# A decoder layer's long convolution: taps loaded once for two units, part of its products in three reduced-precision parts, and GpSimd's sum one unit later

## The reference

```python
x = x + attention(layernorm(x), qkv_w, qkv_b, out_w, out_b, sinks)
q_ = layernorm(x).reshape(B, T, 512) seen as (batch, 32 heads, 8, 512); k_ = v_ = ctx likewise
kv = einsum('bhil,bhjl->bijhl', k_, v_)
y = irfft(rfft(kv, 1024) * rfft(ssm_kernel, 1024))[..., :512]     # causal convolution along l
out = einsum('bijhl,bhil->bjhl', y + kv * D[head], q_)
x = x + out
x = x + (layernorm(x) @ sum_r factors[r]) / sqrt(8) + bias
```

## Time and profile before

| | us |
|---|---|
| median of 3 runs (1989.84 to 1991.06) | 1990.8 |
| time of the profiled execution | 1991.15 |
| its span in the trace | 1989.3 |
| PE busy in the span | 1945.1 |
| DVE busy | 1549.4 |
| ACT busy | 932.2 |
| POOL busy | 826.0 |

### The profile page before, as it was taken

One profiled execution on the slowest core, in us unless ns is written; L12 is line 12 of the kernel. 1 busy time (PEld: TensorE's weight loads), 2 busy tenths in 40 slices (PEclk: granted clock), 3 DMA queues, 4 the chain that ended last, 5 costly groups with the idle time before them and its releaser, 6 DMA issues.

```text
span 1989.3 us, 44846 instructions
## 1 busy us (share of the span) xinstructions
PE 1945.1 (98%) x15500; PEld 1601.7 (81%) x15500; DVE 1549.4 (78%) x4948; ACT 932.2 (47%) x3481; POOL 826.0 (42%) x947
## 2 busy tenths in 40 slices
PE   6899999999999999999999999999999999999899
PEld 6688888888888888888888888888887777777687
DVE  5777777777777777777777777777777899999887
ACT  4554555555555555555555555555544222222333
POOL 3444434333333333333333333333332666666554
PEclk9999999999999999999999999999999999999999
DMA  6146211111112122121111111111104533333343
GB/s 213 46 118 142 72 54 55 65 54 55 55 54 75 44 97 76 55 89 62 54 55 54 54 54 55 54 65 54 54 33 167 183 103 93 93 93 93 106 142 121
DMA packets 71538, 162.20 MB, mean 82 GB/s; under 512 B 6656, under 2 KB 15232, under 8 KB 71184
## 3 DMA queue, kind: packets, MB, share of 16 engines
q1 hardware_dynamic: 62720, 142.48, 21.4%
q0 software_dynamic: 3840, 8.39, 2.3%
q10 hardware_dynamic: 4752, 8.46, 1.1%
HBM read 108.96 MB, written 50.41 MB: 80 GB/s over the span
## 4 chain that ended last, share of the span: by engine, by line
PE 91%; DVE 3%; issue 2%; ACT 2%; POOL 1%; DMA 0%; DVEq 0%; SPq 0%; ACTq 0%; POOLq 0%
PE banks L534 22%; PE banks L596 18%; PE banks L1180 16%; PE banks L573 9%; PE banks L549 9%; PE banks L559 6%; PE banks L1408 5%; PE banks L527 4%; ACT pr L673 1%; PE banks L484 1%; PE banks L1398 1%; PE banks L473 1%; PE banks L1392 1%; DVE pr L891 1%; DVE m L867 0%
## 5 line engine op out<-in xcount | busy, mean ns | idle before, releaser
L673 ACT ACTIVATE pr<-pr,mx 128x128 f32<-128x128 f32 x1024 | 399.0, 391 | 353.1 <-DVE mx L891 353.0
L752 POOL TENSOR_TENSOR m<-m,rope_sb 128x512 f32<-128x512 f32 x160 | 206.3, 1289 | 513.9 <-ACT m L660 513.9
L534 PE MATMUL banks<-xTh,wh 128*128 128x256 f32 x1280 | 376.4, 294 | 2.3 <-DVE xTl L851 1.4
L534 PE MATMUL banks<-xTl,wh 128*128 128x256 f32 x1280 | 363.0, 284 | 0.0
L534 PE MATMUL banks<-xTh,wl 128*128 128x256 f32 x1280 | 362.6, 283 | 0.0
L1180 PE MATMUL banks<-kv,tap 128*128 128x288 f32 x1280 | 318.4, 408 | 4.3 <-issue 1.5
L1180 PEld LDWEIGHTS banks<-kv,tap 128*128 128x128 f32 x1280 | 238.1, 190 | 83.9 <-issue 23.3
L534 PEld LDWEIGHTS banks<-xTh,wh 128*128 128x128 f32 x1280 | 246.2, 192 | 4.0 <-DVE xTl L851 1.8
L900 DVE TENSOR_TENSOR den<-ac,es 128x4 f32<-128x4 f32 x256 | 51.7, 202 | 253.9 <-ACT es L676 253.7
L534 PEld LDWEIGHTS banks<-xTl,wh 128*128 128x128 f32 x1280 | 246.5, 193 | 0.0
L534 PEld LDWEIGHTS banks<-xTh,wl 128*128 128x128 f32 x1280 | 246.1, 192 | 0.0
(11 more groups left out here) (110 smaller groups left out, 3825.6 us busy)
## 6 DMA issues: line engine op xcount, KB each, us to landing
tap<-padded_taps SPq DMA_DIRECT2D x64, 256.0 KB, 3.3
kk<-in_ctxt SPq DMA_DIRECT2D x64, 192.0 KB, 3.4
x_in<-in_x SPq DMA_DIRECT2D x16, 512.0 KB, 3.8
xt_split<-xTh SPq DMA_DIRECT2D x16, 512.0 KB, 2.6
xt_split<-xTl SPq DMA_DIRECT2D x16, 512.0 KB, 3.6
xb<-in_x SPq DMA_DIRECT2D x16, 512.0 KB, 4.6
factors<-in_factors POOLq DMA_DIRECT2D x8, 1024.0 KB, 8.6
x_part_rows<-x SPq DMA_DIRECT2D x16, 512.0 KB, 3.0
```

The lines of the kernel that those rows point to most:

```text
L534: last = pe.matmul(bank[:, h * T:(h + 1) * T], w[:, n, c, h * P:(h + 1) * P], a[:, s, c, :], start=(c == 0 and i == 0), stop=(c == KD - 1 ...
L673: act.activation(pr[:, s, a, cols], pr[:, s, a, cols], ACT.Exp, bias=mx[:, s, i:i + 1], scale=-1.0, accum_out=ac[:, s, i:i + 1])
L752: pool.tensor_tensor(m2[:, s], m2[:, s], rope_sb[:, 1 if i == 0 else 0, 1:3], ALU.mult).then_inc(sin_ready, 1)
```

## The change

- The units are put in another order. The first 6 units (`ALONE`) are heads 0 to 5 of the first batch half; then come 52 units in which each of the heads 6 to 31 is done for the first half and right behind it for the second; the last 6 are heads 0 to 5 of the second half. The 52 are the split units.
- Two split units of a head form a group and use one load of taps; load and buffer go by group. For a split group three DMAs are issued: float32 taps for the off-diagonal blocks (384 columns, 192 KB), and a high and a low part of all four blocks (256 KB each).
- In a split unit each of the 4 diagonal products becomes three float32r products: high taps by high pairs, high by low, low by high. The other 6 stay float32.
- The parts of the taps are made once, during attention: ScalarE copies the taps (128 x 160) into float32r, GpSimd subtracts, SyncE writes three images to DRAM. The parts of chunk 0 of `kv` are made per unit: ScalarE copies 128 x 288 (`pairs_high`), GpSimd subtracts (`pairs_low`), and TensorE waits for it.
- GpSimd's loop runs `pairs(u + 2)`, `last_sum(u - 1)`, `pairs_low(u + 2)`; ScalarE's runs `fetch(u + 1)`, `pairs_high(u + 2)`, `place(u - 1)`.
- The second half's queries are needed from unit 7 on: 12 batch rows are loaded in `first_loads`, two behind the loads of unit 4 and one each behind those of units 5 and 6.
- `pr` moves to another place of SBUF, and the mix waits for `finished` counts (57 and 64) in place of 32 and 64.

```diff
+ALONE = 6
...
-            sp.dma_start(tap0[:, 0:1], ssm_pad[:, P - 1:P], allow_slow_non_contiguous=True).then_inc(tap_in, 16)
-            sp.dma_start(tap0[:, 1:2], dcoef).then_inc(tap_in, 16)
-            sp.dma_start(pad_dram, ssm_pad).then_inc(tap_in, 16)
+            sp.dma_start(taps[:], ssm_pad).then_inc(tap_in, 16)
+            sp.dma_start(through[:], dcoef).then_inc(tap_in, 16)
...
-            if y.number == 1:
-                sp.wait_ge(tap_added, 1)
-                sp.wait_ge(tap_in, 48)
-                sp.dma_start(pad_dram[:, P - 1:P], tap0[:, 0:1], allow_slow_non_contiguous=True).then_inc(tap_out, 16)
+            if y.number == 2:
+                sp.wait_ge(tap_lo, 1)
+                for i, part in enumerate((taps[:], tap_h[:].bitcast(F32), tap_l[:].bitcast(F32))):
+                    sp.dma_start(pad_dram[i], part).then_inc(tap_out, 16)
...
+                if y.number == 1 and p == 0:
+                    act.wait_ge(tap_added, 1)
+                    act.copy(tap_h[:], taps[:]).then_inc(tap_hi, 1)
...
+                if y.number == 1 and p == 2:
+                    pool.wait_ge(tap_hi, 1)
+                    pool.tensor_tensor(tap_l[:], taps[:], tap_h[:].bitcast(F32), ALU.subtract).then_inc(tap_lo, 1)
...
+    order = [(0, h) for h in range(ALONE)] + [(bg, h) for h in range(ALONE, CH) for bg in range(NBG)] + \
+            [(1, h) for h in range(ALONE)]
...
+        h, g = order[u][1], group[u]
+        if u != opening[g]:
+            return
+        if g > 1:
+            sp.wait_ge(conv_done, opening[g - 1])
+        whole = D - P if split(u) else D
+        sp.dma_start(tap[:, g % 2, 0:whole], diagonals(0, h, whole)).then_inc(tap_landed[g % 2], 16)
+        if split(u):
+            for i, part in ((1, tap_hi), (2, tap_lo)):
+                sp.dma_start(part[:, g % 2].bitcast(F32), diagonals(i, h, D)).then_inc(tap_landed[g % 2], 16)
...
-        for b in range(BG):
+        for b in range(BG + BG // 2):
             load_queries(sp, b)
...
+            for b in {4: (12, 13), 5: (14,), 6: (15,)}.get(u, ()):
                 load_queries(sp, b)
...
+    def pairs_high(act, u):
+        act.wait_ge(kv_ready, u + 1)
+        act.copy(kv_hi[:, u % 2], kv[:, u % 2, 0, :]).then_inc(kv_hi_ready, 1)
+
+    def pairs_low(pool, u):
+        pool.wait_ge(kv_hi_ready, u - ALONE + 1)
+        pool.tensor_tensor(kv_lo[:, u % 2], kv[:, u % 2, 0, :], kv_hi[:, u % 2].bitcast(F32),
+                           ALU.subtract).then_inc(kv_lo_ready, 1)
...
-            if u < NCU - 1:
-                last_sum(pool, u)
+            if u > 0:
+                last_sum(pool, u - 1)
+            if split(u + 2):
+                pairs_low(pool, u + 2)
...
-            if u < NCU - 1:
-                place(act, u)
+            if split(u + 2):
+                pairs_high(act, u + 2)
+            if u > 0:
+                place(act, u - 1)
...
+        if split(u):
+            pe.wait_ge(kv_lo_ready, u - ALONE + 1)
         wait(pe, one_added, u - 1)
...
+                if c == d and split(u):
+                    for n, (a, b) in enumerate([(tap_hi, kv_hi), (tap_hi, kv_lo), (tap_lo, kv_hi)]):
+                        last = pe.matmul(y[:, s, c, 0:NY], a[:, k, block], b[:, s], start=(d == 0 and n == 0), stop=(n == 2))
```

More of the change, by code:

```diff
@@ L97, in __init__ @@
         self.fsum = self.tables + 6 * T + 2 * GS * HD
-        words = self.fsum + KD * D
+        self.probs = self.fsum + KD * D
+        self.pairs = self.probs + 8 * T
+        words = self.pairs + 4 * NY
         ctx.enter_context(nc.sbuf_tensor("arena", [P, words], F32))
@@ L164, in attention_part @@
     rs2 = sb("rs2", [P, NT])
-    tap0 = sb("tap0", [CH, 2])
+    taps = sb("taps", [P, TW])
+    tap_h = sb("tap_h", [P, TW], F32R)
+    tap_l = sb("tap_l", [P, TW], F32R)
+    through = sb("through", [P, 1])
     sP = space.banks[:, 0:GS]
@@ L187, in attention_part @@
     tap_added = sem("tap_added")
+    tap_hi = sem("tap_hi")
+    tap_lo = sem("tap_lo")
     x_landed = sem("x_landed")
@@ L813, in body @@
                 if y.first and p == 7:
-                    pool.wait_ge(tap_in, 48)
-                    pool.tensor_tensor(tap0[:, 0:1], tap0[:, 0:1], tap0[:, 1:2], ALU.add).then_inc(tap_added, 1)
+                    pool.wait_ge(tap_in, 32)
+                    pool.tensor_tensor(taps[:, P - 1:P], taps[:, P - 1:P], through[:], ALU.add).then_inc(tap_added, 1)
+                if y.number == 1 and p == 2:
+                    pool.wait_ge(tap_hi, 1)
+                    pool.tensor_tensor(tap_l[:], taps[:], tap_h[:].bitcast(F32), ALU.subtract).then_inc(tap_lo, 1)
         bodies(body)
@@ L1032, in conv_part @@
     terms = space.at("terms", space.moving + 5632, 2, KD, 5 * 8 * BG)
+    tap_hi = space.at("conv_tap_hi", space.probs, 2, D, dt=F32R)
+    tap_lo = space.at("conv_tap_lo", space.probs + 2 * D, 2, D, dt=F32R)
+    kv_hi = space.at("kv_hi", space.pairs, 2, NY, dt=F32R)
+    kv_lo = space.at("kv_lo", space.pairs + 2 * NY, 2, NY, dt=F32R)
     big = space.queries
@@ L1040, in conv_part @@
     kv_ready = sem("kv_ready")
+    kv_hi_ready = sem("kv_hi_ready")
+    kv_lo_ready = sem("kv_lo_ready")
     qs_ready = sem("qs_ready")
@@ L1047, in conv_part, with split, taps_landed, diagonals @@
     NQK, NV = 2 * B * (QM + 1), 2 * B
-    def where(u):
-        return u // CH, u % CH, u % 2
+    order = [(0, h) for h in range(ALONE)] + [(bg, h) for h in range(ALONE, CH) for bg in range(NBG)] + \
+            [(1, h) for h in range(ALONE)]
+    group = [g for g in range(ALONE)] + [ALONE + i // NBG for i in range(NBG * (CH - ALONE))] + \
+            [CH + g for g in range(ALONE)]
+    opening = [group.index(g) for g in range(CH + ALONE)]
+    finished = [max(u for u in range(NCU) if order[u][0] == bg) + 1 for bg in range(NBG)]
+    def where(u):
+        return order[u][0], order[u][1], u % 2
+    def split(u):
+        return ALONE <= u < NCU - ALONE
+    def taps_landed(u):
+        g = group[u]
+        return 16 * sum(3 if split(opening[k]) else 1 for k in range(g % 2, g + 1, 2))
+    def diagonals(i, h, columns):
+        return bass.AP(tensor=pad_dram.tensor, offset=(i * CH + h) * PADW, ap=[[1, P], [1, columns]])
     def wait(eng, s, value):
@@ L1170, in products @@
         s = u % 2
-        pe.wait_ge(tap_landed[s], 16 * (u // 2 + 1))
+        k = group[u] % 2
+        pe.wait_ge(tap_landed[k], taps_landed(u))
         pe.wait_ge(kv_ready, u + 1)
+        if split(u):
+            pe.wait_ge(kv_lo_ready, u - ALONE + 1)
         wait(pe, one_added, u - 1)
@@ L1179, in products @@
             for d in range(c + 1):
-                last = pe.matmul(y[:, s, c, 0:NY], tap[:, s, d * P:(d + 1) * P], kv[:, s, c - d, :],
-                                 start=(d == 0), stop=(d == c))
+                block = slice(d * P, (d + 1) * P)
+                if c == d and split(u):
+                    for n, (a, b) in enumerate([(tap_hi, kv_hi), (tap_hi, kv_lo), (tap_lo, kv_hi)]):
+                        last = pe.matmul(y[:, s, c, 0:NY], a[:, k, block], b[:, s], start=(d == 0 and n == 0), stop=(n == 2))
+                else:
+                    last = pe.matmul(y[:, s, c, 0:NY], tap[:, k, block], kv[:, s, c - d, :],
+                                     start=(d == 0), stop=(d == c))
         last.then_inc(conv_done, 1)
@@ L1254, in conv_part @@
     Conv = namedtuple("Conv", "first_loads more_loads first_pairs first_queries first_products second_products first_sums "
-                              "last_sums last_result last_place sync tensor scalar gpsimd vector")
+                              "last_sums last_result last_place finished sync tensor scalar gpsimd vector")
     return Conv(first_loads, more_loads, first_pairs, first_queries, first_products, second_products, first_sums,
-                last_sums, last_result, last_place, sync, tensor, scalar, gpsimd, vector)
+                last_sums, last_result, last_place, finished, sync, tensor, scalar, gpsimd, vector)
 def mix_part(nc, ctx, space, conv, x1_dram, bias, out, x1_stored, out_done, qk_done, qr_ready, f_in, one_added, res_placed):
@@ L1388, in tensor @@
                     pe.wait_ge(one_added, NBG * CH - 1)
-                pe.wait_ge(res_placed, CH * (b // BG + 1))
+                pe.wait_ge(res_placed, conv.finished[b // BG])
                 wait(pe, x2_ready, v - 1)
```

17 lines of the change are left out of this document (8 added, 9 removed).

## The result

The changed kernel takes 1985.26 us (median of 12 runs, 1984.65 to 1986.19) beside 1989.93 us for the kernel before (12 runs beside them): 4.7 us less, a ratio of 0.9976 with a 95% interval of 0.9967 to 0.9985. The forecast was 6.4 us less, 1984.4 us.

What follows compares the result with a forecast made beforehand. The prediction took a TensorE-VectorE loop over one half of PSUM as the bound, not TensorE's arithmetic. Loop -8.8 us plus start +2.4 us gave -6.4 us, 1984.4 us against the median; 8 of 10 range 1977 to 1992 us.

Steps and rivals of the forecast that it cites:

- The loop over one half of PSUM: TensorE and VectorE in turn on one half: 4.85 us per unit instead of 5.02, 8.8 us less over 52 units.
- One rival's size: Hand-overs shrink too and VectorE becomes the bound at 4.67 us per unit: 18 us gained, 1975 us; chance 0.08.
- The sign that VectorE would idle: In the profile after: VectorE idle 0.1 to 0.3 us before its first terms of every unit, released by the products.
- Products: Diagonal blocks on TensorE: three float32r products take 0.40 us in place of 0.485, saving 0.34 us per unit.
- GpSimd's chain: Pairs, sum and low part end 4.45 us after the products, hidden by 0.5 us; rival where it waits: 1999 us, chance 0.10.
- The sentence that the later sum is where the order counts: GpSimd's sum before the low part is of unit u-1, already finished by VectorE, so GpSimd doesn't stand waiting.
- Taps: 704 KB per pair of units, sent two units (9.7 us) ahead: hidden in the middle of the stage, no charge.
- The rival by which sharing brings the gain: From the float32-again run: shared taps and GpSimd's later sum bring the gain, 4.85 us per unit, about 1985 us; no chance given.
- The start of the split units: Thin DMA cover around units 5 to 7: 2.4 us charged once, bounds 0 and 5 us.
- The sum: Whole kernel: -8.8 + 2.4 = -6.4 us, 1984.4 us against the median; faster by over 0.2% given 0.70.
- The rival in which TensorE's pauses cost the clock: Split units: TensorE's granted clock falls to 0.83, 5.34 us per unit, +17 us, 2010 us; chance 0.03.
- The likeliest case: Whole kernel: -6.4 us, chance 0.66, its own range 1980 to 1988 us.

Runs made afterwards that it cites:

- Four sizes of TensorE's work: Changed kernel with diagonal products all float32 again (1991.5 us), as four float32r (1999.8 us), as three (the change, 1985.26 us), as two (1970.9 us).
- the cut sum in the old kernel: Kernel before the change, with only VectorE's last sum cut into chunk 0 and chunks 1 to 3, TensorE starting behind the first: 1985.37 us, ratio 0.9972.
- two products: Changed kernel without the low taps by high pairs product in each diagonal block, so the result lacks that part: 1970.9 us, 4.576 us per unit.
- the eased kernel: Changed kernel with tap parts of the first two groups loaded ahead and the context of u+1 issued ahead of query rows: 1981.35 us, ratio 0.9952.
- the kernel with the contexts ahead: Changed kernel with only the contexts issued ahead of query rows, unit 6's taps still going out when unit 4 is done: 1983.79 us, ratio 0.9969.
- With GpSimd never idle: Changed kernel with GpSimd doing the low part's subtraction three times, twice into a spare tile: 2024.1 us, 5.590 us per unit.

## Why the prediction was right, and where it was off

- *The loop over one half of PSUM* was forecast at 4.85 us per unit and is 4.842. Its two parts were right too, so this is not luck: from a unit's weights to VectorE's terms it takes 4.88 us (1592.52 to 1597.40; forecast 4.92), and from there to the next weights of the same half 4.78 us (to 1602.18; forecast 4.67 + 0.11). Four sizes of TensorE's work (units of 5.019, 5.116, 4.842, 4.576 us) lie on its line of one half, with the reserve on the outer two given above, and the cut sum in the old kernel moves it without touching TensorE's work. One rival's size was off: VectorE alone needs 4.58 us per unit (two products), not 4.67. The sign that VectorE would idle 0.1 to 0.3 us before the terms of every unit came otherwise: 0.39 us before one unit and nothing before the next in the timeline of 1597 to 1603 us.
- *Products.* Three float32r records of 288 columns last 0.39 to 0.41 us in the chain above (forecast 0.40), except the first three of a unit, behind a pause, with 0.63; the two of a float32 product last 0.48.
- *GpSimd's chain.* Forecast 4.45 us from the end of the products, hidden by 0.5 us; the low part ended 0.53 us before VectorE. Its duration of 0.80 us and ScalarE's 0.43 us were right. The sentence that the later sum is where the order counts is half right: put back with the low part behind it, it costs 41 us; put back with the low part ahead of it, about nothing.
- *Taps* in the middle of the stage: hidden, as forecast. The rival by which sharing brings the gain is out.
- *The start of the split units* is the term that was mis-sized: 2.4 us forecast (bounds 0 and 5), 3.9 measured (12.57 - 10.04, and 15.94 against 14.55 in the eased kernel). The step that failed is the landing of unit 6's third tap load. I gave it the 4.0 to 4.9 us of a single load from the earlier trace rows and called it up to 1 us late; it took 6.57 us in the chain of waits, behind 448 KB of its own group and beside a query row, and unit 6 came 2.0 us late. I had added the bytes ahead for `kk` but not for the taps. Unit 5's 0.6 us, from two query rows ahead of its `kk`, was described and not charged. Unit 7 lost 1.4 us, where I had put all 2.4.
- *The sum.* 52 units at 0.18 us give 9.2 us, less 3.9 is 5.3; the trace shows 5.05 and the medians 4.7. The forecast of 6.4 was too high by the start's 1.5 us. "Faster by over 0.2%" came out narrowly, at 0.24% with an interval from 0.15 to 0.33%.
- *Clock.* The rival in which TensorE's pauses cost the clock didn't come: with 0.15 us of pause per unit (7.25 us in the 49.6 units of the long stretch; by the distances of records, as the forecast counted, it is 4.84 - 4.51 = 0.33 us) the row shows 1.00. What the Trainium skill (TensorE: Matmul & The Clock Gate, section "A second HAM failure mode: psum-queue depth-cycling") reports of a kernel that pauses briefly between its groups of products didn't come at pauses of this size. In the changed kernel's convolution only behind the stall of 2.4 us before unit 6 did it fall, to 0.83 in that stretch of 10 us, in the one execution that was profiled; in the kernel with the contexts ahead a stall as long at the same place left it at 1.00. What decided between the two stays open. Its part in the loss is small: unit 7 started at 1577.77 us, and the low part that it needed was ready only at 1577.43 us, because of the late `kk`; that leaves at most 0.34 us for the clock.
- *The range.* The likeliest case was given 1980 to 1988 us; the bounds of its two terms (6.2 to 13 us, 0 to 5 us) make 1977.8 to 1989.6. The measured 1985.26 us lies in both.

Not tried: leaving a half of PSUM to TensorE right behind VectorE's terms. VectorE's scratch for the sums lies in the same banks.

## What to carry to other kernels

A TensorE that is busy 98% can still be waiting: compare the work of a round (records times their distance) with its period, and look whether two engines that hand a double buffer to and fro close a loop. If they do, the period is half of the sum of their times as long as neither engine alone needs more than that, work saved on either counts half, and the cheapest cut may be to hand over a piece earlier. When a pipeline changes its mode, look at its first rounds one by one: there the loads have one period of cover where they later have two, and each load lands behind all that was issued just ahead of it.

## What the runs showed of the hardware

- Three float32r products of 288 columns take 0.39 to 0.41 us, one float32 product 0.48 to 0.49. Float32r saves 18% where it needs three, and 45% with two (0.133 us each, from the 0.53 us that the third one's four records took off a unit).
- In the records a float32r product behind a float32 one seems long and early: the first of the three has a mean of 474 ns, the others 294. Only sums over a group can be trusted. Groups by line of the changed kernel, 1590 to 1830 us:

```profile
L1244 PE MATMUL banks<-kv_hi,conv_tap_hi 128*128 128x288 f32 x194 | 92.0, 474 | 7.2 <-DVE terms L1304 6.3
...
L1244 PE MATMUL banks<-kv_hi,conv_tap_lo 128*128 128x288 f32 x194 | 57.1, 294 | 0.0
```

- With GpSimd never idle, each of its records is 0.07 to 0.08 us longer than in the change (0.87 against 0.80 us, 2.33 against 2.25), while the distance from L1160 to L1162, 2.22 us, stays that of the earlier trace rows (2.21). The added length is overlap of records, not work.
